# Second attention's end in a graph kernel: norms moved ahead of the last rows, transposes moved into their predecessor's products

## The reference, cut to what matters

```python
h = gat_conv(x, edge_index, W1, a_src1, a_dst1, b1, HEADS, HID, True)   # four heads, 1024 columns
h = layer_norm(h, g1, be1)
h = jax.nn.relu(h)
h = h + (h0 @ Wr1 + br1)
h1 = h
h = gat_conv(h, edge_index, W2, a_src2, a_dst2, b2, 1, OUT_DIM, False)   # starts with h1 @ W2
h = layer_norm(h, g2, be2)
h = h + (h1 @ Wr2 + br2)
```

## Time and profile before

| | |
|---|---|
| median of 3 runs | 1198.71 us (1198.4 to 1199.52) |
| the profiled execution | 1199.95 us, its span 1198.1 us |
| PE busy | 1083.9 us (90%) |
| DVE busy | 993.6 us (83%) |
| ACT busy | 655.0 us (55%) |
| POOL busy | 147.6 us (12%) |
| the last rows of the second attention | up to 868.6 us |
| gemm2, twenty passes | 883.4 to 1071.6 us |
| third attention | up to the end |

### The profile page before, as it was taken

How to read it: one execution, slowest core, us unless ns; L and a number is a source line. 1 busy time by engine, 2 the same in 40 slices (tenths; PEclk the granted TensorE clock), 3 DMA queues, 4 the chain that set the end, 5 groups by cost and what they waited for, 6 DMA issues and landing times.

```text
span 1198.1 us, 20786 instructions
## 1 busy us (share of the span) xinstructions
PE 1083.9 (90%) x7873; PEld 909.4 (76%) x7873; DVE 993.6 (83%) x1698; ACT 655.0 (55%) x1070; POOL 147.6 (12%) x155
## 2 busy tenths in 40 slices
PE   5988669988888988699999999999979999999996
PEld 2543546666666666599999899999978888788885
DVE  6888899999999999796785699999897765277864
ACT  6443789999998999522300276676711311232431
POOL 1000000000000000000028020120510015321111
PEclk9999779999999999899999999999989999999998
DMA  4011302020202020552244701203041114245111
GB/s 139 27 53 52 132 1 87 1 87 1 87 2 87 6 87 1 190 187 95 79 128 140 252 28 38 79 2 117 26 176 59 36 66 176 69 146 186 66 64 49
DMA packets 39858, 98.94 MB, mean 83 GB/s; under 512 B 4467, under 2 KB 17147, under 8 KB 39765
## 3 DMA queue, kind: packets, MB, share of 16 engines
q1 hardware_dynamic: 39766, 97.66, 23.8%
HBM read 70.74 MB, written 26.90 MB: 81 GB/s over the span
## 4 chain that ended last, share of the span: by engine, by line
PE 60%; DVE 25%; issue 10%; ACT 3%; DVEq 1%; POOL 1%; DMA 1%; POOLq 0%; ACTq 0%
PE psum L921 14%; PE psum L1004 13%; DVE R L1534 12%; PE psum L969 11%; PE psum L1032 9%; DVE R L1520 6%; PE psum L954 3%; PE psum L700 3%; PE psum L985 1%; DVE LC L1498 1%; PE psum L804 1%; DVE R L1400 1%; PE psum L1015 1%; DVE R L1399 1%; ACT R L1153 1%
## 5 line engine op out<-in xcount | busy, mean ns | idle before, releaser
L863 PE MATMUL psum<-ident,R 128*128 128x128 f32 (+3 forms) x1200 | 158.8, 281 | 49.9 <-ACT R L1153 49.5
L863 PEld LDWEIGHTS psum<-ident,R 128*128 128x128 f32 (+3 forms) x1200 | 129.1, 143 | 90.9 <-ACT R L1153 80.7
L1534 DVE CUSTOM_DVE_ANT_0 R<-R,LC 128x1250 f32<-128x1250 f32 x120 | 175.4, 1463 | 0.0
L1153 ACT ACTIVATE R<-R,row_max 128x1250 f32<-128x1250 f32 x120 | 161.4, 1345 | 5.5 <-DVE row_max L1534 4.0
L877 PE MATMUL psum<-R 128*64 128x256 f32 (+3 forms) x1200 | 148.5, 386 | 0.0
L1169 ACT COPY R<-psum 128x1280 f32<-128x1280 f32 x120 | 143.3, 1194 | 1.5 <-PE psum L863 1.5
L921 PE MATMUL psum<-w_hi,x1T_hi 128*128 128x256 f32 (+1 forms) x480 | 136.0, 283 | 2.2 <-issue 1.5
L921 PE MATMUL psum<-w_lo,x1T_hi 128*128 128x256 f32 (+1 forms) x480 | 135.0, 281 | 0.0
L921 PE MATMUL psum<-w_hi,x1T_lo 128*128 128x256 f32 (+1 forms) x480 | 134.8, 281 | 0.0
L1520 DVE SCALAR_TENSOR_TENSOR R<-R 128x1250 f32<-128x1250 f32 x80 | 122.1, 1526 | 0.0
L1980 POOL TENSOR_TENSOR rstd<-rstd,minus_half 128x1 f32<-128x1 f32 (+1 forms) x40 | 32.0, 801 | 720.0 <-DVE rstd L1547 720.0
(11 more groups left out here) (223 smaller groups left out, 2613.1 us busy)
## 6 DMA issues: line engine op xcount, KB each, us to landing
R<-rows_spill SPq DMA_DIRECT2D x20, 625.0 KB, 5.3
rowbuf<-rows_spill SPq DMA_DIRECT2D x14, 625.0 KB, 5.1
lc_spill<-LC SPq DMA_DIRECT2D x9, 625.0 KB
LC<-lc_spill SPq DMA_DIRECT2D x9, 625.0 KB, 5.9
res_spill<-colbuf SPq DMA_DIRECT2D x36, 128.0 KB, 2.0
R<-res_spill SPq DMA_DIRECT2D x9, 512.0 KB, 3.5
R<-in_x_dram SPq DMA_DIRECT2D x1, 3456.0 KB
res_spill<-R SPq DMA_DIRECT2D x9, 384.0 KB
```

What stands on the lines that cost most here:

```text
L863: last = e.transpose(turn0[r % 2][0:m, s, 0:n_dst], ring[0:n_dst, r % RING0, s * P:s * P + m], ident[0:n_dst, 0:n_dst])
L1153: e.activation(ring[0:m, r % RING0, :], ring[0:m, r % RING0, :], ACT.Exp, bias=row_max[0:m, r % RING:r % RING + 1], scale=-1.0, accum_out= ...
L1534: e.tensor_tensor_reduce(slot, slot, LC[0:m, i, :], 1.0, MIN_CEILING, ALU.add, ALU.min, row_max[0:m, r % RING:r % RING + 1]).then_inc(S.le ...
```

## The change

DVE: h_stats(0) is done in pass r = 34, h_norm(0) in r = 36 ahead of least1(39), h_stats(1) in r = 37; h_norm(1) and h_stats(2) come behind rest_h1(0). POOL: the power for tile 0 comes behind W2's rest k = 2; rest k = 6 waits for the last least1, k = 7 for the last recip1. PE: gemm2(v) is cut in two halves of 24 products, with turn_h1(v+1) between them, in all passes but the last; gemm2(0) waits for each rest of W2 as it needs it, and no longer for the last finish1.

```diff
-            def gemm2(v):
+            def gemm2(v, ks):
                 i = v % NT
                 m = rows[i]
                 his, los = (w2_hi, w2_lo) if v < NT else (wr2_hi, wr2_lo)
-                e.wait_ge(S.h1T_lo, v + 1)
-                if i == 0:
-                    e.wait_ge(S.wr2_lo if v else S.w2_lo, KH)
-                if v < 2:
-                    e.wait_ge(S.h_conv, ROWS1)
-                elif v < NT + 2:
-                    e.wait_ge(S.xl2, v - 1)
-                else:
-                    e.wait_ge(S.base, v - 1 - NT)
-                for k in range(KH):
+                if ks[0] == 0:
+                    e.wait_ge(S.h1T_lo, v + 1)
+                    if v == NT:
+                        e.wait_ge(S.wr2_lo, KH)
+                    if v == 1:
+                        e.wait_ge(S.h_conv, ROWS1)
+                    elif 2 <= v < NT + 2:
+                        e.wait_ge(S.xl2, v - 1)
+                    elif v >= NT + 2:
+                        e.wait_ge(S.base, v - 1 - NT)
+                for k in ks:
+                    if v == 0:
+                        e.wait_ge(S.w2_lo, k + 1)
                     for step, (hs, ws) in enumerate(((h1T_hi, his), (h1T_hi, los), (h1T_lo, his))):
                         for c, w in halves:
                             last = e.matmul(acc2[v % 2][0:m, c:c + w], hs[v % 2][:, k, 0:m], ws[k][:, c:c + w],
                                             start=(k == 0 and step == 0), stop=(k == KH - 1 and step == 2))
-                last.then_inc(S.gemm2, 1)
+                if ks[-1] == KH - 1:
+                    last.then_inc(S.gemm2, 1)
...
             for v in range(2 * NT):
                 if v + 1 < 2 * NT:
+                    gemm2(v, range(KH // 2))
                     turn_h1(v + 1)
+                    gemm2(v, range(KH // 2, KH))
                 else:
                     e.wait_ge(S.h1T_lo, 2 * NT)
                     turn_exp2(0)
-                gemm2(v)
+                    gemm2(v, range(KH))
...
+                if r == ROWS1 - 6:
+                    h_stats(0)
                 if r == ROWS1 - 4:
-                    h_stats(0)
+                    h_norm(0)
                 if r == ROWS1 - 3:
-                    h_norm(0)
                     h_stats(1)
-                if r == ROWS1 - 2:
+
+
+            for v in range(2 * NT):
+                rest_h1(v)
+                if v == 0:
                     h_norm(1)
                     h_stats(2)
-
-
-            for v in range(2 * NT):
-                rest_h1(v)
                 if v + 2 < NT:
                     h_norm(v + 2)
...
             for k in range(KH):
                 e.wait_ge(S.w2_hi, k + 1)
                 e.wait_ge(S.leaky1, min(NT * (H1 - 1) + 7 + k, ROWS1))
+                if k == KH - 2:
+                    e.wait_ge(S.least1, ROWS1)
+                if k == KH - 1:
+                    e.wait_ge(S.recip1, recips1(ROWS1 - 1) + 2)
                 e.tensor_tensor(w2_lo[k], w2_raw[k], w2_hi[k].bitcast(F32), ALU.subtract).then_inc(S.w2_lo, 1)
-            for i in range(NT):
+                if k == W2_EARLY - 2:
+                    norm_power(NT, 0)
+            for i in range(1, NT):
                 norm_power(NT + i, i)
```

## The result

The kernel after took **1204.45 us** (median of 11 runs, 1201.81 to 1206.75); the kernel before took 1199.49 us beside it (11 runs, 1197.38 to 1202.31). The ratio is 1.0038, with a 95% interval of 1.0025 to 1.005: slower by more than 0.2%. The forecast was 1204.0 us, with a range of 1197 to 1208 and 0.64 for slower. The profiled execution of after took 1206.6 us, its span is 1204.8 us.

A forecast was written before the change was run, and what follows sets the result against it. PE, busy nearly everywhere, was taken as the bound, its idle time deciding. Terms 2.8 (head) - 2.5 (rows) + 3.6 (last pass) + 1.4 (clock) = +5.3 gave 1205.2 us profiled, hence 1204.0 as median; range 1197 to 1208.

The forecast's parts named there:

- The head, as far as h_norm(0): End of attention: h_norm(0) runs from 860.9 to 868.0, turn_exp1(39) comes at 871.1, PE idles 6.5 us.
- two rests of 1.55 each: POOL's W2 rests k=4 and k=5 each hold h_norm(0) on DVE by 1.55 us; 3.3 with k=3's tail.
- Rival 1: POOL's rests hold h_norm(0) by nothing: +2.0, 1200.7 us, or 1197.9 if the clock survives too; chance 0.22.
- The clock in the head: PE's idle time before turn_exp1(39) lowers the clock, which costs 2.8 us.
- The new stall before gemm2(1): gemm2(1) waits 2.7 us as rest_h1(1) stands behind norms and statistics on DVE; no clock fall.
- The head's sum: Up to the end of gemm2(1), at 904.0 instead of 901.2: +2.8 us.
- Transposes amid products: 0, no stall.: Steady gemm2 passes: turns between the halves cost 0 (bounds -0.5 and +0.5), and DVE and ACT cause no stall.
- The rows: At turn_h1(16) and turn_h1(17), the waits for keep_row2 vanish: -2.5 us, bound 0.
- The last pass: Before turn_exp2(0): turn_h1(19) behind 24 products delays exp2(0), +3.6 us, bounds 2.5 and 4.6.
- The clock in the tail: The 3.6 us gap before turn_exp2(0) may lower the clock: half of 2.8, +1.4 us, bounds 0 and 2.8.

The follow-up runs named there:

- e2_rests_late: Kernel after, but POOL's W2 rests k = 4 and 5 also wait for the last least1; 1202.1 us, ratio to before 1.0016.
- e8_reordered: Kernel after, but h_norm(0) in row 37, one norm less ahead, no cut in passes 9 to 14 and from 17, dot products spread; 1189.89 us, ratio 0.9917.
- e7_dots_first: Kernel after, but POOL's additions of biases wait for DVE's dot products of eight tiles; 1201.79 us, one run.
- e10_turn18_ahead: Kernel after, but turn_h1(18) goes ahead of all of gemm2(17), turn_h1(19) staying amid gemm2(18); 1203.54 us, one run.
- e1_tail_ahead: Kernel after, but turn_h1(19) goes ahead of all of gemm2(18), other passes still cut; 1206.29 us, ratio to before 1.0038.
- e5_tail_two_ahead: Kernel after, but turn_h1(18) and turn_h1(19) both go ahead of their whole gemm2; 1199.94 us, ratio to before 1.000.
- e6_rows_early: Kernel after, but turn_h1(19) ahead of all of gemm2(18) and SP stores and reloads the score rows one step earlier; 1206.44 us, one run.
- e4_head_only: Kernel after with only its DVE and POOL parts: gemm2 whole, each turn_h1(v+1) ahead of gemm2(v); 1201.99 us, ratio to before 1.0016.

## Why the prediction was right, point by point

**The head, as far as h_norm(0).** h_stats(0) began at 849.33 (forecast 849.25), h_norm(0) at 860.41 (860.9), it took 6.9 us (7.1), turn_exp1(39) came at 870.32 (871.1), the gap was 5.92 (6.5). The term that a neutral reading leaves out, two rests of 1.55 each, was the right one: e2_rests_late took it away and 2.96 us went. Rival 1, no collision, is excluded by that.

**The clock in the head: too dear.** From turn_exp1(39) to gemm2(0) I had 9.0 + 2.8 = 11.8 us; it was 10.7. Without a fall (e8_reordered) this stretch took 9.8, and 0.46 of it were two short waits. So the fall costs about 1.4 here, not 2.8, and my 9.0 was 0.3 short. The 2.8 came from a place where use1(39) was slow too; here only turn_exp1(39), use1(38) and the start of what follows lay in it.

**The new stall before gemm2(1).** Forecast 2.7, measured 2.66. That the clock survives it held in this execution and in four of the seven others with such a gap (below).

**The head's sum.** At the point that I forecast, the end of gemm2(1), it was +1.3 us instead of +2.8: 902.6 instead of 904.0. turn_exp1(39) came 0.8 earlier than I had it, the stretch to gemm2(0) was 1.1 shorter, and gemm2(0), the stall and gemm2(1) together took 21.6 us instead of 21.1. The term that was mis-sized is the clock's.

**"Transposes amid products: 0, no stall."** This step failed. I had taken DVE's longest pass as 8.6 us, from v = 6, and hadn't asked what shifts against POOL when a pass of DVE moves by 4.2 us, and by the head's loss on top. One gap of 1.08 us came of it, and with the passes around it 1.4 us between the ends of gemm2(9) and gemm2(14); e7_dots_first took 0.9 us of it away. The cuts themselves cost nothing elsewhere: from the end of gemm2(1) to that of gemm2(9) it is 73.66 us in after and 73.63 in before.

**The rows.** The 2.5 us went, as forecast, and 0.35 us beside them; no wait for rowbuf is left.

**The last pass.** The gap was 4.26 us, 3.6 forecast. rest_h1(19) to exp2(0) took 6.05 us in after, exactly as in before (1054.48 to 1060.53), so the 0.4 us that I had rest_xl2(5) gain weren't there. The mechanism held, e10_turn18_ahead shows it alone; but I had one chain where a second, over turn_h1(18) and the rows' transfer, was only 0.75 us shorter, and a third stood behind it. Anyone who repaired the kernel by my text would have got e1_tail_ahead, which is no faster.

**The clock in the tail: too cheap.** I took half of 2.8. It fell in every kernel with a gap of 3.7 us or more there, and stayed up behind 1.40 and 1.86; from turn_exp2(0) to the first use2 it took 13.34 us in after against 10.85 in before: 2.5 us, within the bounds. In the other kernels with the fall it was 12.0 to 13.0.

**On the whole.** Between the profiled executions the terms are 5.3 - 1.5 (head) + 1.4 (middle) - 0.3 (rows) + 0.6 (last gap) + 1.1 (clock in the tail) = 6.6 us; between the medians it is 5.0. The medians hold more executions, and the clock may fall elsewhere in them; that isn't shown. The sign rested on two mechanisms, the hold by POOL and turn_h1(19) behind the products, and both stood. That the number came so near is luck in part: the head's loss was forecast 1.5 us too large, and what lies behind it 2.8 us too small.

## What to carry to other kernels

Moving an operation later by half a pass moves everything that it releases, on each engine and each DMA queue: follow every chain from it to the next deadline, and ask of each pass of DVE which of POOL's operations it now meets. When an experiment frees the chain you named and the gap stays to a tenth, there is a second chain of nearly the same length: free them one by one, and each alone. A wait that a trace shows at the end of a chain may be what keeps two engines apart; compare durations, not only start times, before you take it away. And when an edit moves work across a mark, take another mark: by the starts of the passes the head would seem to cost 0.4 us here (gemm2(1) began at 38.35 against 37.97), and by their ends, where the same work is done, it costs 1.3.

## What the runs showed of the hardware

- Where POOL and DVE meet, both get longer. An operation of DVE with two SBUF inputs ran at 2.4 to 3.1 us instead of 0.96 to 1.5 whether it was short or long (0.96 to 2.48, 1.28 to 2.75, 1.46 to 2.99, 1.51 to 3.10), that is, by 1.5 us for each, and POOL's 128x768 addition at 2.56 to 3.03 instead of 1.84. The price goes by the number of meetings, not by the length of the DVE operation. One that met only the end of a POOL operation lost less: 1.48 instead of 1.28 us at 860.41 and 1.99 instead of 1.46 at 855.40 in after. An operation with one input from PSUM was not held.
- A gap of 2.6 to 2.7 us before or amid the first passes of gemm2 left the clock at 1.00 in after, e5_tail_two_ahead, e6_rows_early, e7_dots_first and e10_turn18_ahead (gemm2(0) to gemm2(10): 95.07 to 95.09 us in all five), and brought it to 0.5 in e1_tail_ahead and e2_rests_late (96.62 in both) and in e4_head_only. The three that fell ran on the same chip; whether it is the chip, I can't tell. The price of the fall is 1.55 us in the first two. The stretch behind that gap, in e1_tail_ahead:

```profile
894.00:896.00 2.00, 2.00 (x9) 1.66 (x8) 1.97 (x2) 0.00 (x0) 0.00 (x0) 0.55 0.78 310
```
